# Twelve value blocks moved from the context projection into the state space stage, and the state space kernel built in the projection

## The reference

```python
x = x + _L1_xattn_ref(_layernorm(x), ctx_1024, fside, ...)   # 16 heads of 16, a bias of 128 x 12544 a head
x = x + _L1_attn_ref(_layernorm(x), Win, bin_, A_log, B, C, Dp, dt, Wout, bout)
x = x + _L1_ffn_ref(_layernorm(x), Wg, bg, We, be)
x = x + _L2_xattn_ref(_layernorm(x), ctx_1024, Wq, Wk, Wv, Wo)   # 16 heads of 64
...
# _L1_attn_ref
x = x @ Win.T + bin_
u = transpose(x)
logdA = -exp(-A_log) * dt[:, None]
powers = exp(logdA[:, :, None] * t)                 # 256 channels x 64 states x time
k = einsum('dn,dnl->dl', C * (B * dt[:, None]), powers)
y = causal_convolution(u, k) + u * Dp[:, None]      # the reference goes by an FFT
return transpose(y) @ Wout.T + bout
...
# _L2_xattn_ref: the values are the same whatever x is
k = context @ Wk;  v = context @ Wv;  attn = softmax(q k / 8);  out = (attn v) @ Wo
```

## Time and profile before

| | us |
|---|---|
| median of three runs | 3363.52 |
| lowest, highest | 3355.19, 3363.97 |
| profiled execution, its own time | 3362.06 |
| its span | 3360.3 |
| TensorE busy | 3062.3 (91%) |
| VectorE busy | 1485.1 (44%) |
| ScalarE busy | 1453.5 (43%) |
| GpSimd busy | 246.9 (7%) |
| moved by DMA | 576.42 MB, mean 172 GB/s |

### The profile page before, as it was taken

One profiled execution on the slowest core, in us unless ns is written; L12 is line 12 of the kernel. 1 busy time (PEld: TensorE's weight loads), 2 busy tenths in 40 slices (PEclk: granted clock), 3 DMA queues, 4 the chain that ended last, 5 costly groups with the idle time before them and its releaser, 6 DMA issues. The chain is left out here.

```text
span 3360.3 us, 66618 instructions
## 1 busy us (share of the span) xinstructions
PE 3062.3 (91%) x23749; PEld 1948.1 (58%) x23749; DVE 1485.1 (44%) x4104; ACT 1453.5 (43%) x2501; POOL 246.9 (7%) x178
## 2 busy tenths in 40 slices
PE   8999999998787999995699999999999887999989
PEld 4555555556475666663445555555555675666678
DVE  2222222221424788885433333333333225888632
ACT  2323222223222888883144444444444432565621
POOL 2313232220000000000000000000000002000000
PEclk9999999999897999997899999999999987999979
DMA  6787878878238999970611111111111244665355
GB/s 212 255 257 255 252 257 248 257 243 277 86 120 312 357 353 356 356 309 21 241 40 39 57 57 38 57 57 38 57 57 38 83 165 120 154 155 146 98 180 197
DMA packets 298888, 576.42 MB, mean 172 GB/s; under 512 B 75522, under 2 KB 245288, under 8 KB 287528
## 3 DMA queue, kind: packets, MB, share of 16 engines
q1 hardware_dynamic: 298804, 575.31, 50.9%
HBM read 394.29 MB, written 180.97 MB: 171 GB/s over the span
## 5 line engine op out<-in xcount | busy, mean ns | idle before, releaser
L1558 DVE TENSOR_SCALAR_CACHE_REDUCE all_S<-l2x_scores 128x448 f32<-128x448 f32 x448 | 261.0, 619 | 413.7 <-PE l2x_scores L1473 413.7
L1460 PE MATMUL l2x_key_bank<-l2x_ctxT,l2x_wk_cur 128*64 128x448 f32 x1792 | 386.2, 552 | 3.0 <-DVE l2x_q_all L1602 1.4
L339 PE MATMUL prep_work<-prep_wv,prep_ctxT 128*128 128x512 f32 x784 | 341.5, 594 | 0.0
L1622 ACT COPY l2x_keys<-l2x_key_bank 128x448 f32<-128x448 f32 x224 | 119.2, 532 | 488.3 <-PE l2x_key_bank L1460 486.4
L705 DVE CUSTOM_DVE_ANT_0 all_S<-l1x_scores,l1x_bias 128x448 f32<-128x448 f32 x448 | 261.5, 620 | 56.1 <-PE l1x_scores L617 51.6
L960 DVE TENSOR_REDUCE l3x_rowmax<-l3x_scores 128x1 f32<-128x448 f32 x448 | 263.4, 622 | 39.7 <-PE l3x_scores L880 38.1
L1042 ACT ACTIVATE l3x_pT<-l3x_turned 128x896 f32<-128x896 f32 x224 | 205.0, 917 | 169.3 <-PE l3x_turned L888 166.0
L1496 PEld LDWEIGHTS l2x_out<-l2x_pT,l2x_v_half 128*64 128x64 f32 x3136 | 203.5, 137 | 96.7 <-issue 96.5
L774 ACT ACTIVATE all_S<-all_S,l1x_negmax 128x896 f32<-128x896 f32 x224 | 232.9, 1043 | 53.2 <-DVE l1x_negmax L718 33.5
L339 PEld LDWEIGHTS prep_work<-prep_wv,prep_ctxT 128*128 128x128 f32 x784 | 147.9, 190 | 185.4 <-issue 174.1
L1460 PEld LDWEIGHTS l2x_key_bank<-l2x_ctxT,l2x_wk_cur 128*64 128x64 f32 x1792 | 108.9, 136 | 245.2 <-issue 245.2
(11 more groups left out here) (647 smaller groups left out, 4241.3 us busy)
## 6 DMA issues: line engine op xcount, KB each, us to landing
l1x_bias<-in_fside_Bx16xSxS_dram SPq DMA_DIRECT2D x112, 896.0 KB, 6.8
scratch_k<-prep_kparts SPq DMA_DIRECT2D x84, 672.0 KB, 3.3
l1x_k_half<-scratch_k SPq DMA_DIRECT2D x32, 1568.0 KB, 9.6
l2x_v_half<-scratch_v SPq DMA_DIRECT2D x32, 1568.0 KB, 6.3
l3x_k<-scratch_k SPq DMA_DIRECT2D x32, 1176.0 KB, 7.3
scratch_v<-prep_st_v SPq DMA_DIRECT2D x14, 2048.0 KB, 9.3
scratch_k<-prep_kparts SPq DMA_DIRECT2D x56, 448.0 KB, 4.6
scratch_v<-prep_st_v SPq DMA_DIRECT2D x14, 1536.0 KB, 7.2
```

The lines of the kernel that those rows point to most:

```text
L339: last = nc.tensor.matmul(w[:, h, :], ctxT[:, k, j * P:(j + 1) * P], wv2[:, k, h * 512:(h + 1) * 512], start=(k == 0), stop=(k == KT - 1))
L1460: last = nc.tensor.matmul(keys_ps[half * VW:(half + 1) * VW, 0:HB], wk_cur[:, k, :], ctxT[:, k, (2 * c + half) * HB:(2 * c + half + 1) * H ...
L1558: nc.vector.tensor_scalar(com.S[:, b * HB:(b + 1) * HB], scores_ps[half][:, 0:HB], 1.0, -3.4e38, ALU.mult, ALU.max, accum_out=rowmax[:, b: ...
```

## The change

Groups 0 and 1 of the projection are written out and use a short plan that ends after block 0 of the wide values: twelve value blocks are left out. The other twelve groups stay a loop. The left-out blocks are made in the state space stage: 24 half blocks by TensorE while VectorE convolves, copied by ScalarE, and stored by SP in four stores; the first piece of the turned context is loaded for this at the end of layer 1's attention, the value weights (1 MB) again in the stage. The convolution's weights are loaded at the end of layer 1's attention too, and the 50 filling matmuls are gone. The steps of `StateKernel` go from the heads of layer 1's attention into the twelve long groups of the projection, ten a group, and eight at its end. The context pieces of layer 2's attention are loaded in three stages instead of one, and some of its small tiles lie in the weights' tiles. Two phases more enclose these stages.

```diff
+LATE = 2
+N_LATE = LATE * (GC - 1)
...
+class ContextAhead:
...
+        self.piece = [ph.sb("ctx0", [P, KT, 2 * GW])]
...
+    def load(self, sp, pieces):
+        for i in pieces:
+            sp.dma_start(self.piece[i][:, :, :],
+                         self.scr.ctxT[:, :, i * 2 * GW:(i + 1) * 2 * GW]).then_inc(self.loaded[i], 16)
...
+        short, all_steps = plan[:10], plan
...
+        FRONT_AT = {"v": 7, "s": 6}
+        STEPS_AT = {"s": {10: range(0, 5), 12: range(5, 10)}, "v": {11: range(0, 5), 13: range(5, 10)}}
...
+        def each_group(engine, one):
+
+            for g in range(LATE):
+                one(g, short)
+            with engine.Fori(LATE, GRP) as g:
+                one(g, plan)
...
-                    for i, (c0, c1) in enumerate(WIDE):
-                        for c in (c1 - 2, c1 - 1):
+                    for i, (c0, c1) in enumerate(wide):
+                        for c in range(max(c0, c1 - 2), c1):
...
-                with sp.Fori(0, GRP - 1) as g:
+                states.on_sync(sp)
+                for g in range(LATE):
                     load(g + 1)
-                    store(g)
-                store(GRP - 1)
+                    store(g, ((0, 1),))
+                with sp.Fori(LATE, GRP - 1) as g:
+                    load(g + 1)
+                    store(g, WIDE)
+                store(GRP - 1, WIDE)
...
+                            for step in STEPS_AT["v"].get(i, ()):
+                                states.vector_step(dve, g - LATE, step)
...
+                            for step in STEPS_AT["s"].get(i, ()):
+                                states.scalar_step(act, g - LATE, step)
...
+                states.rest(states.vector_step, dve, GRP - LATE)
...
         for c in range(GRP):
-            if beside is not None:
-                beside.vector_step(dve, h, c)
...
-            if beside is not None:
-                beside.scalar_step(act, h, c)
...
                 run.on_sync(sp)
+                if load_next is not None:
+                    load_next(sp)
...
-                for i in range(GRP // 2):
-                    cols = slice(i * 2 * GW, (i + 1) * 2 * GW)
-                    sp.dma_start(ctxT[:, :, cols], scr.ctxT[:, :, cols]).then_inc(ctx_loaded[i], 16)
+                ahead.load(sp, (4, 5, 6))
...
-def l1_state_space(nc, com, a):
+def l1_state_space(nc, com, a, weights, ahead):
...
+                sp.dma_start(wv2[:, :, :], a["L2_xattn_Wv"].rearrange("(k p) n -> p k n", p=P)).then_inc(wv2_loaded, 16)
+                ahead.load(sp, (1, 2, 3))
+                for i in range(LATE):
+                    for c in (0, 3):
+                        n = i * (GC - 1) + c
+                        sp.wait_ge(value_taken, (n + 3) * 2)
...
-                keep_busy(nc, com, misc_ps, 50)
-                pe.wait_ge(loaded, 80)
+                pe.wait_ge(loaded, 64)
...
+                for n, (i, c, half) in enumerate(pieces):
+                    if n >= 3:
+
+                        pe.wait_ge(value_taken, n - 2)
+                    at = (i * GC + c) * P
+                    for k in range(KT):
+                        last = nc.tensor.matmul(value_ps[n % 3][:, :], ahead.piece[0][:, k, at:at + P],
+                                                wv2[:, k, half * 512:(half + 1) * 512],
+                                                start=(k == 0), stop=(k == KT - 1))
...
+                for n in range(len(pieces)):
+                    act.wait_ge(value_full, n + 1)
+                    half = n % 2
+                    nc.scalar.copy(late[:, half * 8:(half + 1) * 8, n // 2, :],
+                                   value_ps[n % 3][:, :].rearrange("p (h e) -> p h e", e=64)).then_inc(value_taken, 1)
...
+        with phase(nc, "early") as ph:
+            weights, ahead = StateSpaceWeights(nc, ph, a), ContextAhead(nc, ph, scr)
...
+            cross_attention_16(nc, com, a, scr, "L1", load_next)
+            with phase(nc, "ahead") as ph:
+                ahead.add_pieces(ph)
+                l1_state_space(nc, com, a, weights, ahead)
+                l1_experts(nc, com, a)
+                l2_cross_attention(nc, com, a, scr, ahead, [weights.nat[m][:, :, :].rearrange("p k n -> p (k n)")
+                                                            for m in ("in", "out")])
```

More of the change, by code:

```diff
@@ L1179, in cross_attention_16 @@
[L1179 removed]
+def cross_attention_16(nc, com, a, scr, layer, load_next=None):
     n = layer.lower()
@@ L2482, in l1_state_space @@
         products = ph.sb("products", [P, RING, KT, P])
+        wv2 = ph.sb("wv2", [P, KT, HEADS * 64])
+        late = com.S[:, 0:N_LATE * HEADS * 64].rearrange("p (h n e) -> p h n e", h=HEADS, n=N_LATE)
+        value_ps = [ph.ps(f"value{i}", [P, 512]) for i in range(3)]
         turned_ps = [ph.ps(f"turned{i}", [P, 512]) for i in range(2)]
```

281 lines of the change are left out of this document (164 added, 117 removed).

## The result

The changed kernel takes 3322.93 us in the median of four runs (3318.68 to 3326.69), against 3363.74 us for the kernel before (3355.19 to 3366.89, four runs): a ratio of 0.9882, with a 95% interval of 0.9861 to 0.9904, 40.8 us less. The forecast was 3320 us in a range of 3297 to 3340. The profiled execution took 3318.68 us (span 3317.0), the lowest of the four.

The account below looks back on a forecast made before the run. TensorE bounds the projection, three engines in turn layer 1's attention, VectorE's convolution the state space stage. -27.6 - 1.3 - 12.1 - 2.0 + 1.2 = -41.8 on 3362.06 gives 3320 us, range 3297 to 3340.

Parts of the forecast that it names:

- item 1: Projection, groups 0 and 1: twelve value blocks leave, 41.6 us less for TensorE, groups shrink from 54.85 to 34.1 us.
- item 2: Projection, junctions into groups 1 and 2: ScalarE waits for a late key store and TensorE stops; +14 us (0 to 20).
- The queue walk: Projection, short groups: transfers taken in series on SP's queue; narrow stores land at 48 us, next key store at 61.5.
- item 3: Projection, long groups: ten state steps each (0.40 us each on ScalarE) hide under TensorE's value blocks; cost 0.
- item 4: Layer 0's attention: the exponential's table is already loaded from the projection, so its 1.28 us load goes; -1.3 us.
- item 5: Layer 1's attention: without state steps heads save 12, last head 2.2, start 0.5; table loads cost 2.6; together -12.1 us.
- item 6: State space stage: value blocks run beside the convolution, output product ends at 1608.3 instead of 1610.3; -2.0 us (-3.5 to +2).
- item 7: Boundary after layer 2's attention: two more phases clear semaphores, +1.2 us; layer 1's experts and layer 2's attention 0.
- A: Projection: no stall, 3306 us, and with layer 1's heads at their lower bound 3296; 20%.
- B: Projection junctions and layer 1's heads: transfers bind more, 10 us at each junction, nothing gained from heads; 3338 us; 18%.
- C: From the state space stage on: TensorE's clock stays low, 3389 us, 4%; half (value blocks alone, 82.6 us) 3361, 4%.
- D: State space stage: the value blocks are projected but not hidden, because their copies wait; 2%, counted with the half of C.

Follow-up runs that it names:

- run 5: The changed kernel with the last late value store issued behind the expert weights' loads; layer 1's experts took 21.8 us (28.4 in the changed kernel).
- run 7: The changed kernel with 140 filling matmuls instead of 40 in layer 1's experts, the store left in place; that stage took 27.1 us.
- run 10: The changed kernel loading half of each bias tile from layer 1's second head on; 431.8 us from first to last maximum (431.9 in the changed kernel).
- run 1: The changed kernel with the short groups' narrow stores cut to a seventh; the two junctions cost 2.2 and 2.1 us, 4.3 against 14.2.
- run 2: The changed kernel with four tiles for the split keys instead of two; junctions cost 3.9 and 2.1 us, the projection took 820.0 us.
- run 11: The changed kernel with four split-key tiles, table load ahead of the loop, last late store behind expert weights, value weights first in halves; 3309.31 us.
- run 8: The changed kernel without any state step; long groups took 54.86 to 54.88 us (54.87 or 54.88 in the changed kernel).
- run 3: The changed kernel with a small exponential ahead of layer 1's head loop, loading the table there; 429.4 us from first to last maximum, 2.5 less.
- run 4: The changed kernel with 90 filling matmuls instead of 40 in layer 1's experts; that stage took 28.5 us.
- run 6: The kernel of run 5 with 90 filling matmuls instead of 40 in layer 1's experts; that stage took 24.1 us.

## Why the prediction was right, point by point

- *Twelve blocks leave (item 1).* Right: group 0 takes 34.09 us, 34.1 forecast. (In runs 5, 7 and 10 it took 35.8, its first matmuls at half clock.)
- *What comes late (item 2).* The size was right (14.2 us, and 11.5 to 15.9 in eight more profiles, +14 forecast), the step that led to it was half wrong, so the size is partly luck. The prediction let ScalarE wait once, for the key store, and TensorE pay it in full. The wait is there at the forecast place, and is worth 2 us a junction by itself (run 1). The other one the prediction didn't price: the store of the narrow values still holds their tile when the next group's copy comes. With the clock that it costs it is the larger by itself, 3.9 and 2.1 us in the two junctions of run 2, 5.9 and 4.3 in run 11. The two don't simply add up: in group 2 together they made 7.7. The queue walk had that landing (48 us) and the next group's need of it in the same numbers; I read only one of the two users off it. And the clock: all three gaps of 2.3 us and more on TensorE at these junctions were followed by matmuls at half speed, which the sum had at nothing.
- *State steps in the projection (item 3).* Right: nothing (run 8). They were even shorter than taken, 0.31 us and not 0.40 each on ScalarE.
- *Layer 0's table load (item 4).* Right: 1.3 forecast, and from the row maximum to the exponential it is 0.19 us instead of 1.43, 1.2 less.
- *Layer 1's heads (item 5).* 15 heads with their table loads gave 7.7 us, 9.4 forecast; without the loads 10.2 (run 3: 439.6 - 429.4), 12 forecast: 0.68 a head and not 0.8. The loads cost 2.5 us, 2.6 forecast, and lie where it said, in one head of four; the last head gave 2.3 (39.7 to 37.4 us from its maximum to the next norm), 2.2 forecast. The start of the stage gave 0.2, 0.5 forecast (43.9 to 43.7 us from the norm to the first maximum). With the drain that the Trainium skill ("ScalarE: Activation LUTs", What ACT_TABLE_LOAD costs) adds to a load, three loads would take 8 us, by an estimate from its figures; run 3 measured 2.5, and in the trace the next exponential starts 1.29 us after a load does.
- *State space stage (item 6).* Right in this profile (-1.9), but about zero over the others (51.5 to 54.9, 53.4 before), so the -2.0 was met by luck. The step "the value weights land beside the norm" failed: they came 1.5 us too late here and up to 2.4 elsewhere, and the blocks began at 7.5 us into the stage and not at 6.6. The larger part of the spread is the clock of the first blocks, for which the sum allowed 1 us: in seven of ten profiles it cost 1.7 to 2.9.
- *The experts and the boundaries (item 7).* Wrong: "0" was +5.8 us. The forecast let the late stores "end under the next stage" and forgot who else is on the queue there. The last one is still in the queue as that stage asks for its weights, which land 1.9 us later (6.2 us after the start instead of 4.3); TensorE falls to half clock, and the remaining 4 us are that. That the store is the cause of both is shown by run 5; the split between them is read off the traces. The boundary's +1.2 was 0.7 at its own place (TensorE's idle time of 1.68 us grew to 2.40). But layer 2's attention as a whole was -0.6 only in this profile, and +1.5 to +3.4 in the other eleven. TensorE's one wait for a transfer there is for the query weights (0.4 us), none for the late stores or a context piece, so that sign of being wrong did not show.
- *Rivals.* A (no stall) is refuted by the group times. B is refuted in both halves: its 20 us at the junctions by the 11.5 to 15.9 measured, and the heads bound by transfers by run 10: the 358 GB/s of the Trainium skill ("DMA: Bandwidth & Descriptors", Specifications) is no wall here, the 400 us of the changed kernel moved 362 GB/s at a share of 0.91. C (the clock stays low) is refuted in its size: the value blocks took 41.4 to 44.3 us in all twelve profiles, and not 82.6. But a low clock under the first blocks was there in eight of them, and at half clock TensorE lost time one stage later as well. That the lost filling causes either is not shown. D is refuted, the blocks are hidden.

The total (-40.8 in the medians of the runs, -43.3 in the spans of the two profiles, -41.8 forecast) is partly luck. In this profile the error of +5.8 in the experts met four stages that the forecast had at nothing and that were short (l0a and l0f, l2a, l3a: -9.0 together), and short draws in the state space stage and in layer 2's attention. With the median of the profiles of the same code for each stage that the change touches, the differences from the kernel before are about -29.4 (projection and layer 0's attention), -10.3, 0.0, +4.7 and +2.4: -32.6 in place of the -41.8. Where the rest of the 40.8 us comes from can't be said with a single profile of the kernel before.

## What to carry to other kernels

When work is moved from a full engine to an idle one, follow its transfers too: the bytes that it leaves behind in the old place (here narrow stores in a group that has become shorter than its queue) and those that it brings to the new one (a last store that stands before the next stage's weights) gave back about half of the 41 us that the moved matmuls had saved, 14.2 and 5.8 us. Of one late landing, list all its users, the first one pays. An instruction that needs a table, taken out ahead of a loop, can move the table's load into the loop.

## What the runs showed of the hardware

- In the changed kernel's profile, gaps of 2.3 to 3.8 us on TensorE, at the junctions and in the experts, were each followed by some us of work at 0.50 (1.2 GHz). It is no rule: in run 2 the matmuls behind a gap of 2.45 us went at 0.50 and those behind one of 2.40 us (the row below) at 1.00. After gaps of 1.8 to 1.9 us in the experts it went both ways too (run 5 kept 1.00, run 4 fell). More filling matmuls ahead of a gap did not keep the clock (runs 4, 6, 7).

```profile
110.31 2.86 PE L506 MATMUL prep_work<-prep_T_v,prep_ctxT 128*128 128x256 f32 x12 [2.40 <-ACT prep_st_v L542]
```

- One core drew up to 404 GB/s over ten us with the DMA engines at a share of 1.02, and 430 GB/s over four while the context pieces were loaded beside the convolution, the first window under the value blocks above.
- Stages of the same code differed between profiles by 3 us (l2a) to 7 us (l3a), and the projection by 6 us, all of it in its start, its first three groups and its end: the long groups, in which TensorE hardly waits, took 54.86 to 54.89 us in all twelve profiles.
